# Twenty transposes of the identity matrix on TensorE before the first tile of a two-layer attention and expert kernel

## The chip, the core and the metric

The kernel runs on one core of one Trainium2 chip. The metric is the device time of one execution in microseconds (us); less is better. The times given are medians of several executions, and the profile is of one further execution whose own time is given beside them.

The core has five engines with an instruction stream each: TensorE (PE; its weight loads are shown as PEld), VectorE (DVE), ScalarE (ACT), GpSimd (POOL) and SyncE (SP), which here only issues transfers. The engines wait for one another through semaphores.

## The reference, cut to what matters

Four batches of 256 rows of 256 numbers (`x`) pass through two layers. Each layer adds a cross attention over a context of 1601 rows per batch and then a feed-forward step:

```python
x = x + L0_xattn(layernorm(x), ctx, mask)          # softmax(x @ ctx.T / 16, masked) @ ctx
x = x + L0_ffn(layernorm(x), Wr, Wg, Wu, Wd)       # 8 experts, the best 2 of each row
x = x + L1_xattn(layernorm(x), W_qkv, W_o, ..., ctx, ctx, 54)   # keeps the 54 largest scores of a row
x = x + L1_ffn(layernorm(x), w1, w2)               # rows and weights rounded to few levels
```

Everything is float32 but the last step's products, which are of small integers.

## The kernel before

The 1024 rows are 8 tiles of 128, two tiles to a batch. All work is cut into named steps, and one hand-made list, `ORDER`, gives the order in which they are issued; each engine's block walks the same list (`STEPS`) and issues the steps that are its own. So each engine's order is fixed, and what it does next waits for semaphores alone.

The first steps of the list are the place of this case. SP issues `ldx.0` (x of tiles 0 and 1, L448), the four pieces of the first batch's transposed context (`ldk.1.0.0` to `ldk.1.0.3`, L464, tile `k_sb`, one of 402, two of 400 and one of 399 columns), the other three pairs of x tiles and then the context rows `v_sb` (L480). POOL writes the constants, the identity matrix `ident` among them (L497 to L525), and adds to the semaphore `consts` after each. DVE takes the mean and variance of the first two tiles (`stats`, `aggr`, `var`: L990, L996, L1002), POOL raises the variance to -1/2 (`rstd`, L534) and DVE writes the normalized rows `xn` (`norm.1.0`, L1015). TensorE transposes `xn` into a PSUM bank (`xT.1.0`, L811, tile `T`, four transposes), ACT copies that out (`xTe`, L593), and TensorE multiplies it with the context.

These products are the steps `s1.t.c` (L826): tile t of x with piece c of `k_sb`, into one of the two banks `S`. One such step is two products of 128x128 by 128x400, each of which the trace shows as two MATMUL instructions, so it has four. DVE takes a bank out with the mask added and the row's maximum (`s1e`, L1026, tiles `row` and `mx1c`); after that the bank is free for the step after the next. Ahead of its first `s1e` DVE's order has the statistics of all other x tiles (`stats.1.3`, `stats.1.1`, `stats.1.2`, and what follows them), and between `s1e.0.0` and `s1e.0.1` it has `norm.1.1`.

TensorE's block begins with a wait for all constants (`pe.wait_ge(consts, N_CONSTS)`), and then walks the list. The bank `O_bank` (tile `O`) is first used by `router.0` (L867), tens of us later, whose product overwrites it.

Of the kernel before, what the change touches and what calls it, by code (L numbers as in the profile page):

```python
# [18 lines left out]
P = 128  # L19
# [192 lines left out]
def two_layers(nc, x, ctx, ctxT, mask, Wr, Wg, Wu, Wd, WqT, WoT, beta_q, beta_k, gate, log_tau, w1T, w2T, out):  # L212
    es = ExitStack()
    with es:
        def sb(name, shape, dt=F32):
            return es.enter_context(nc.sbuf_tensor(name, shape, dt))
# [34 lines left out]
        ident = sb("ident", [P, P])  # L251
# [68 lines left out]
        def bank(name):  # L320
            return es.enter_context(nc.psum_tensor(name, [P, 512], F32))
# [3 lines left out]
        O_bank = bank("O")  # L325
# [412 lines left out]
        def _(pe):  # L738
# [59 lines left out]
                    pe.wait_ge(aTe_done, n("aTe", before_t))  # L798

            pe.wait_ge(consts, N_CONSTS)  # L800
            for step in STEPS:
                op, key = step[0], step[1:]
                if op == "xT":
# [544 lines left out]
```

## Time and profile before

| | |
|---|---|
| median of 3 runs | 454.04 us (453.79 to 455.31) |
| the profiled execution's own time | 452.51 us |
| its span, first to last instruction | 450.8 us |
| mean granted TensorE clock in it | 0.943 of full speed |
| PE busy | 359.8 us (80% of the span) |
| PEld busy | 287.6 us (64%) |
| DVE busy | 306.5 us (68%) |
| ACT busy | 172.7 us (38%) |
| POOL busy | 48.8 us (11%) |

The profiled execution has 1.7 us outside its span. PE is busy nearly all the time in the first 40% of the span, DVE from there to the end. In the chain of waits, which is followed back from the last instruction, PE has 36% of the span, DVE 33%, and transfers 9%.

The granted clock is a share of full speed: 1.00 is 2.4 GHz and 0.50 is 1.2 GHz. Busy time of PE is modelled where matmuls are pipelined: what one MATMUL takes by itself is more than the distance between the starts of two in a row.

### The profile page before, as it was taken

How to read it: one execution, taken by the hardware profiler on the slowest of the kernel's cores; microseconds unless marked ns; L12 is line 12 of the kernel's file. 1: busy time of each engine (PE TensorE's matmuls, PEld its weight loads, DVE VectorE, ACT ScalarE, POOL GpSimd, SP SyncE). 2: the span in 40 equal slices, each digit the busy share in tenths (PEclk: the TensorE clock that was granted, in tenths of full speed). 3: DMA queues.
4: the chain of work that ended last, by engine and by line, in shares of the span. 5: the costliest groups of instructions: out<-in, count | busy, mean ns of one | idle time of the engine just before them, and what ended most of it. 6: DMA issues, size and time to landing. Idle time of an engine off the chain costs nothing.

```text
span 450.8 us, 6595 instructions
## 1 busy us (share of the span) xinstructions
PE 359.8 (80%) x2077; PEld 287.6 (64%) x2082; DVE 306.5 (68%) x776; ACT 172.7 (38%) x294; POOL 48.8 (11%) x100
## 2 busy tenths in 40 slices
PE   0999999997999986399998789579958446567975
PEld 0577776875888775286777678477636336556853
DVE  2623474643201341063999999999999999999994
ACT  2143444432432352043433635315663110551475
POOL 3100000034000006440000000271000000000100
PEclk9999999999899999799999999969996958699899
DMA  7593968239187769763989674433421005144201
GB/s 249 173 310 98 310 224 296 84 103 358 37 281 211 236 229 316 245 224 96 321 258 293 191 231 159 133 107 123 125 68 54 0 0 153 45 142 140 82 15 58
DMA packets 70809, 76.38 MB, mean 169 GB/s; under 512 B 5356, under 2 KB 69496, under 8 KB 70776
## 3 DMA queue, kind: packets, MB, share of 16 engines
q1 hardware_dynamic: 57272, 59.93, 41.6%
q10 hardware_dynamic: 11968, 11.84, 8.0%
q0 software_dynamic: 1536, 4.20, 2.7%
q8 instruction: 17, 0.28, 0.2%
q14 instruction: 16, 0.13, 0.1%
HBM read 66.91 MB, written 9.04 MB: 169 GB/s over the span
## 4 chain that ended last, share of the span: by engine, by line
PE 36%; DVE 33%; issue 12%; DMA 9%; POOL 4%; ACT 4%; SPq 1%; ACTq 1%; POOLq 0%; DVEq 0%
PE S L826 11%; PE GU L904 8%; DVE fold L1190 7%; DVE cand_h L1178 7%; PE A L853 5%; PE O L913 4%; DVE cand_l L1185 4%; DMA xg<-xs 3%; DVE fold L1195 3%; DVE row L1218 3%; DMA xs<-xn,idx_u 2%; POOL xs L544 2%; DMA x_res<-x 2%; PE T L840 2%; DVE gabs L1296 2%
## 5 line engine op out<-in xcount | busy, mean ns | idle before, releaser
L904 PE MATMUL GU<-xgT,ew_ring 128*128 128x128 f32 x480 | 60.9, 281 | 9.1 <-issue 8.1
L857 PE MATMUL A<-pT,v_sb 128*128 128x128 f32 (+1 forms) x416 | 59.3, 304 | 10.2 <-ACT pT L608 5.8
L904 PEld LDWEIGHTS GU<-xgT,ew_ring 128*128 128x128 f32 x480 | 58.1, 196 | 13.7 <-issue 9.1
L857 PEld LDWEIGHTS A<-pT,v_sb 128*128 128x128 f32 (+1 forms) x416 | 56.9, 218 | 13.5 <-issue 7.6
L608 ACT ACTIVATE pT<-T 128x512 f32<-128x512 f32 x64 | 31.8, 514 | 87.6 <-PE T L840 85.7
L840 PE MATMUL T<-ident,row 128*128 128x128 f32 (+1 forms) x208 | 34.9, 302 | 32.3 <-DVE row L1218 27.0
L1178 DVE MAX8 cand_h<-fold 128x8 f32<-128x801 f32 x56 | 54.7, 985 | 0.1
L840 PEld LDWEIGHTS T<-ident,row 128*128 128x128 f32 (+1 forms) x208 | 27.6, 156 | 40.5 <-issue 31.0
L853 PE MATMUL A<-v_sb,pT 128*128 128x256 f32 (+1 forms) x208 | 50.7, 388 | 0.0
L826 PE MATMUL S<-k_sb,xT 128*128 128x400 f32 (+2 forms) x128 | 49.0, 516 | 1.3 <-ACT xT L593 1.1
L826 PE MATMUL S<-k_sb,qT 128*128 128x400 f32 (+2 forms) x128 | 45.8, 503 | 2.6 <-ACT qT L665 2.1
L1190 DVE MATCH_REPLACE8 fold<-cand_h,fold 128x801 f32<-128x801 f32 x48 | 46.9, 978 | 0.0
L1117 DVE TENSOR_TENSOR hid<-hid,GU 128x256 f32<-128x256 f32 x30 | 12.4, 416 | 46.0 <-ACT hid L622 45.9
L853 PEld LDWEIGHTS A<-v_sb,pT 128*128 128x128 f32 (+1 forms) x208 | 39.0, 196 | 6.9 <-issue 0.2
L1026 DVE CUSTOM_DVE_ANT_0 row<-S,mask_add 128x400 f32<-128x400 f32 (+2 forms) x32 | 18.3, 573 | 30.3 <-PE S L826 30.2
L826 PEld LDWEIGHTS S<-k_sb,qT 128*128 128x128 f32 x128 | 23.5, 192 | 18.3 <-ACT gel L704 2.3
L913 PE MATMUL O<-ew_ring,hid 128*128 128x256 f32 x120 | 31.6, 385 | 4.0 <-DVE hid L1117 3.2
L826 PEld LDWEIGHTS S<-k_sb,xT 128*128 128x128 f32 x128 | 23.9, 196 | 16.7 <-issue 3.6
L1185 DVE MAX8 cand_l<-fold 128x8 f32<-128x801 f32 x32 | 31.4, 982 | 0.0
L622 ACT ACTIVATE hid<-GU 128x256 f32<-128x256 f32 x30 | 11.5, 384 | 45.8 <-PE GU L904 45.8
L561 POOL TENSOR_TENSOR rstd<-var,minus_half 128x1 f32<-128x1 f32 x8 | 4.6, 579 | 209.6 <-DVE var L1247 209.6
L676 ACT ACTIVATE row<-S 128x400 f32<-128x400 f32 (+2 forms) x32 | 16.0, 504 | 28.2 <-PE S L826 28.2
(153 smaller groups left out, 469.8 us busy)
## 6 DMA issues: line engine op xcount, KB each, us to landing
v_sb<-ctx SPq DMA_DIRECT2D x36, 512.0 KB, 4.1
ew_ring<-Wg SPq DMA_DIRECT2D x30, 256.0 KB, 3.4
ew_ring<-Wu SPq DMA_DIRECT2D x30, 256.0 KB, 3.9
ew_ring<-Wd SPq DMA_DIRECT2D x30, 256.0 KB, 4.5
k_sb<-ctxT SPq DMA_DIRECT2D x16, 400.0 KB, 4.2
xg<-xs ACTq DMA_DIRECT2D x30, 128.0 KB, 3.6
ys<-y_sb ACTq DMA_DIRECT2D x30, 128.0 KB, 3.3
k_sb<-ctxT SPq DMA_DIRECT2D x8, 402.0 KB, 3.9
```

What stands on the lines that cost most here:

```text
L608: act.activation(pT[0:r, i % NPT, :, :].rearrange("p a s -> p (a s)")[:, 0:w], t_bank("pT", *key)[0:r, 0:w], ACT.Copy).then_inc(pTe_done, 1)
L676: act.activation(row3[:, t % 4, c0:c0 + w], s_bank("s3", t, c)[:, 0:w], ACT.Copy) \
L826: mm = pe.matmul(s_bank(*step)[:, 0:w], lhs[:, k, :], k_sb[:, l // 2, c, k, 0:w], start=k == 0, stop=k == KC - 1)
L840: mm = pe.transpose(t_bank(*step)[0:r, a * P:(a + 1) * P], src[:, m * P:m * P + r], ident[:, :])
L853: mm = pe.matmul(A_bank[:, 0:D], pT[0:r, j, a, :], v[0:r, a, :], start=m == 0, stop=m == NMC - 1)
L857: mm = pe.matmul(A_bank[:, o * P:(o + 1) * P], v[0:r, a, o * P:(o + 1) * P], pT[0:r, j, a, :], start=m == 0 and o == 0, stop=m == NMC - 1 ...
L904: mm = pe.matmul(gu_bank(*key)[:, a * F + f * P:a * F + (f + 1) * P], ew_ring[:, w % NW, a, k, f * P:(f + 1) * P], cols[:, k, :], start=k ...
L913: mm = pe.matmul(O_bank[:, 0:D], hid[:, i % NHID, f, :], ew_ring[:, w % NW, 2, f, :], start=f == 0, stop=f == F // P - 1)
L1026: dve.tensor_tensor_reduce(out=row1[:, t % 2, c0:c0 + w], in0=s_bank("s1", t, c)[:, 0:w], in1=mask_add[:, c0:c0 + w], scale=1.0, scalar=BE ...
L1178: dve.max(cand_h[:, t % 2, 8 * r:8 * r + 8], fold[:, t % 2, 0:HALF]).then_inc(maxH_done, 1)
L1185: dve.max(cand_l[:, t % 2, 1 + 8 * r:9 + 8 * r], fold[:, t % 2, HALF:RW]).then_inc(maxL_done, 1)
L1190: dve.match_replace(part, cand_h[:, t % 2, 8 * r:8 * r + 8], part, BELOW_ALL).then_inc(repH_done, 1)
```

## The change

Between TensorE's wait for the constants and its first step, twenty transposes of `ident` are issued, each with `ident` as the second operand too, all into the first 128 columns of `O_bank`. Nothing reads what they write, they wait for nothing more, and they signal nothing. Every other instruction of every engine is as before and in the same order.

```diff
             pe.wait_ge(consts, N_CONSTS)
+            for _ in range(20):
+                pe.transpose(O_bank[:, 0:P], ident[:, :], ident[:, :])
             for step in STEPS:
```

The head of TensorE's instructions before (S is a bank of scores, T one of transposes):

```order
L811 MATMUL T<-ident,xn 128x128 x4
L826 MATMUL S<-k_sb,xT 128x402 x2
L826 MATMUL S<-k_sb,xT 128x400 x4
L826 MATMUL S<-k_sb,xT 128x399 x2
L826 MATMUL S<-k_sb,xT 128x402 x2
```

And after the change, two lines further down in the file:

```order
L802 MATMUL O<-ident 128x128 x20
L813 MATMUL T<-ident,xn 128x128 x4
L828 MATMUL S<-k_sb,xT 128x402 x2
L828 MATMUL S<-k_sb,xT 128x400 x4
L828 MATMUL S<-k_sb,xT 128x399 x2
```

Only the row at L802 is new. Here a product counts once where the trace shows two MATMULs; a transpose is one in both.

## Rows read from the trace of the kernel before

**Rows 1.** The chain that ended last, its start: start us, us, what.
```profile
4.49 8.73 DMA x_res<-x
...
13.24 1.42 DVE bn L990 x4
...
15.21 1.35 POOL rstd L534 x2
...
16.59 0.74 DVE xn L1015 x2
17.32 0.48 DVE row L1026
...
17.87 6.99 PE S L826 x20
```

**Rows 2.** Timeline of PE: start us, us, line, operation, out<-in, count [idle before <-releaser].
```profile
9.65 1.09 PE L811 MATMUL T<-ident,xn 128*128 128x128 f32 x4 [9.65 <-DVE xn L1015]
11.52 6.17 PE L826 MATMUL S<-k_sb,xT 128*128 128x402 f32 x12 [0.78 <-ACT xT L593]
17.87 6.99 PE L826 MATMUL S<-k_sb,xT 128*128 128x399 f32 x20 [0.18 <-DVE mx1c L1026]
24.70 0.60 PE L811 MATMUL T<-ident,xn 128*128 128x128 f32 x4
...
25.98 1.15 PE L840 MATMUL T<-ident,row 128*128 128x128 f32 x8 [0.25 <-ACT xT L593]
```

**Rows 3.** Timeline of the weight loads (PEld), first score steps.
```profile
12.32 0.34 PEld L826 LDWEIGHTS S<-k_sb,xT 128*128 128x128 f32 x1 [0.33 <-issue]
12.99 0.34 PEld L826 LDWEIGHTS S<-k_sb,xT 128*128 128x128 f32 x1 [0.33 <-issue]
...
14.33 0.34 PEld L826 LDWEIGHTS S<-k_sb,xT 128*128 128x128 f32 x1 [0.33 <-issue]
14.88 0.53 PEld L826 LDWEIGHTS S<-k_sb,xT 128*128 128x128 f32 x2 [0.21 <-issue]
16.08 0.97 PEld L826 LDWEIGHTS S<-k_sb,xT 128*128 128x128 f32 x4 [0.68 <-DVE mx1c L1026]
```

**Rows 4.** Timeline of the other engines, 0 to 24 us.
```profile
1.30 1.86 SPq L464 DMA_DIRECT2D k_sb<-ctxT  x3
...
4.07 0.10 POOL L525 MEMSET row<- 128x4 f32 x1
...
10.77 0.60 ACT L593 ACTIVATE xT<-T 128x512 f32<-128x512 f32 x1 [3.34 <-PE T L811]
...
15.44 0.58 DVE L1026 CUSTOM_DVE_ANT_0 row<-S,mask_add 128x402 f32<-128x402 f32 x1
...
17.24 0.57 DVE L1026 CUSTOM_DVE_ANT_0 row<-S,mask_add 128x400 f32<-128x400 f32 x1
```

**Rows 5.** L811, 9 to 11 us: count, duration ns min/median/max.
```profile
L811 PE MATMUL T<-ident,xn x4: 421/421/447, 9.7 to 10.3; 128*128 128x128 f32 x4
```

**Rows 6.** L811 again, 24 to 26 us.
```profile
L811 PE MATMUL T<-ident,xn x4: 271/272/273, 24.7 to 25.0; 128*128 128x128 f32 x4
```

**Rows 7.** All engines, 9.5 to 14.9 us: busy (count) PE, PEld, DVE, ACT, POOL, clock.
```profile
9.50:14.90 5.40, 4.47 (x10) 2.59 (x11) 2.80 (x12) 0.60 (x1) 0.70 (x1) 1.00 1.08 375
```

**Rows 8.** PE stretches around 366 us: length, busy (count), granted clock, DMA, GB/s.
```profile
359.49:366.32 6.83, 0.00 (x0) 0.50 0.00 0
366.32:369.73 3.41, 2.86 (x13) 0.50 0.00 0
369.73:373.14 3.41, 1.97 (x18) 1.00 0.10 16
```

**Rows 9.** Timeline of PE in the middle one of these stretches.
```profile
366.87 2.89 PE L840 MATMUL T<-ident,row 128*128 128x128 f32 x12 [12.65 <-DVE row L1218]
369.56 2.04 PE L857 MATMUL A<-pT,v_sb 128*128 128x128 f32 x16
```

**Rows 10.** PE stretches around a fall of the clock, and one without.
```profile
414.10:417.52 3.42, 1.61 (x15) 1.00 0.47 146
417.52:420.93 3.41, 3.41 (x16) 0.50 0.03 10
400.45:403.86 3.41, 1.37 (x9) 1.00 0.42 148
403.86:407.28 3.42, 2.01 (x16) 1.00 0.00 0
```

**Rows 11.** Transfers issued in the first 10 us: count, KB, us to landing.
```profile
k_sb<-ctxT SPq DMA_DIRECT2D x2, 400.0 KB, 7.3
```

## What the change should do to the time

> **What bounds the kernel now.** I read the chain of waits first, from its start, since the change acts only there. Its start isn't TensorE's [rows 1]: the chain goes through the transfer of later x tiles (it ends at 4.49 + 8.73 = 13.2 us), DVE's statistics of them, POOL's `rstd`, DVE's second `xn`, DVE's second `row` at 17.32, and only at 17.87 does it pass to PE. From there on PE has twenty MATMULs in a row and then goes on with transposes and products with hardly a gap [rows 1, 2]: an idle time of 0.25 us is all that stands before 25.98. So what happens on PE ahead of 17.87 counts only by what it moves the start at 17.87, and every us that is taken from PE after it is on the path.
>
> Second, PE's own rows show how fast it ran. The first four transposes take a median of 421 ns each, and four of the same shape at 24.7 us take 272 ns [rows 5, 6]. The loads of the first score step start 0.67 us apart (12.32, 12.99, and on to 14.33), while the twenty MATMULs from 17.87 take 6.99 us, or 0.35 each [rows 2, 3]. At 14.88 two loads stand in one row, and that is where the pace changes. PE was therefore at the lower of its two clocks (1.2 GHz) when it began at 9.65, and got the higher (2.4 GHz) near 14.8, after it had multiplied without a break from 11.52. The profile's own figure for the granted clock is 1.00 over this whole stretch [rows 7], from before its first recorded change, and does not show this; the durations do. The change gives PE something to do in a time in which it had nothing (it sat idle for 9.65 us [rows 2]), which could bring that rise forward.
>
> Third, what PE waits for between 15.9 and 17.87. The loads of the third score step wait at 16.08 for DVE's `mx1c`, after 0.68 us of idleness, and the fourth step waits for it again at 17.87 [rows 2, 3]. DVE for its part begins `row` at 15.44 without any idle time before it [rows 4]: it came from the statistics, not from waiting for PE's product.
>
> **The change part by part.** The transposes begin when the last constant is written, at 4.07 + 0.10 us [rows 4], say 4.2. Their pace at the lower clock comes from twelve transposes of this shape at a granted clock of 0.50: 2.89 us in all [rows 8, 9], of which the last one's own length is about 0.43, so (2.89 - 0.43) / 11 = 0.22 us apart. The first tile's four give the same: (1.09 - 0.42) / 3 = 0.22 [rows 2, 5]. Twenty end at 4.2 + 19 x 0.22 + 0.43 = 8.8 us. The first real transposes are released at 9.65 by DVE's `xn` [rows 2]. They are covered by PE's own idleness with 0.85 us left over, and cost nothing. Between the bounds for their cost: at the higher clock eight such transposes take 1.15 us [rows 2], so twenty end by 7.1; if each had to end before the next could begin, at 421 ns apiece, they would end at 4.2 + 20 x 0.42 = 12.6 and hold up the first tile by 3.0 us. I take 0.22, since both rows with transposes in a row at the lower clock show it; what is new here is that all twenty write the same columns, for which no row of transposes stands, though the two halves of a product follow one another into the same columns without a gap. The twenty weight loads are of the same kind as those of the other transposes and are in the 0.22.
>
> What they can give. If the clock is high by 9.65 and stays, the four transposes take 0.60 in place of 1.09 (a gain of 0.5 us) [rows 2], and the five spacings between 11.52 and 14.88 shrink from 0.67 to 0.34 or 0.35, which is 5 x 0.33 = 1.6 us. Together 2.1 us of PE's time. Followed through: transposes end near 10.2, ACT's copy of 0.60 us [rows 4] near 10.9, products start at 11.0, and the eight MATMULs of the first two steps are done by 11.0 + 8 x 0.35 = 13.8 instead of about 15.9. The context pieces are there (the two of 400 columns take 7.3 us to land from issues between 1.3 and 3.2 us [rows 4, 11]).
>
> What becomes of it. At 13.8 both `S` banks are full. The third step needs the first one emptied, which DVE does at 15.44 to 16.0, since it is still waiting for x from memory until 13.2 and then working through it [rows 1, 4]. So PE waits from 13.8 to 16.08 where it waited 0.2 to 0.7 us before; the third step begins at 16.08 as before, the fourth at 17.87 as before, because DVE's second `row` comes after `xn`, which comes after POOL [rows 1]. The 2.1 us are gained ahead of a gate that does not move. Sum on the path: 0.0 us. The profiled execution would stay at 452.5 (450.8 of span and 1.7 around it), and scaled to the median of the runs shown that is 454.04 + 0 = 454.0 us.
>
> **Does a transpose raise the clock at all?** At 366 us the granted clock is 0.50 after 6.83 us with nothing on PE; then twelve transposes run and hardly anything else, and in the next stretch the clock is 1.00 [rows 8, 9]. So a row of transposes has been followed by a rise in this very trace. The Trainium skill, page "TensorE: Matmul & The Clock Gate", section "Part 4: PE-mode transpose", says otherwise: that transposes do not count as PE being busy and that the full clock does not engage for them. By that rule the change would leave the clock as it was and the time at 454.0; by the row the clock rises and the time is, through the gate at DVE, 454.0 too. The row speaks against the rule, though the one or two products at the end of that stretch leave a little room for it.
>
> **The rivals.**
>
> *The clock falls in the new gap, slower.* With the first two steps done at 13.8, PE does nothing from 13.8 to 16.08 and works 1.35 us of the next 1.8. The trace has a stretch with 1.61 us of work in 3.42 after which the clock was 0.50, and one with 1.37 in 3.41 after which it was still 1.00 [rows 10]. Before the change the slower pace itself filled this gap. If the clock falls here, it does so near 16 to 18 us and lasts a stretch such as the 3.41 us at 0.50 in rows 10; PE is then on the path, and a half of that is lost: 1.7 us, so 455.7. It decides from the point at which the low stretch reaches beyond 17.87; one that ends before costs nothing. For it: the gap is 2.3 us long and ends right at the place that counts. Against: it needs the rise to have held from 9 to 13.8 first, over the pauses at 8.8 to 9.65 and 10.2 to 11.0; where the clock falls again in these, PE is back to the pace of before and there is no gap.
>
> *Executions differ, and others lose more at the start, faster.* The profiled execution took 452.51 us, 1.5 less than the median. If in others the rise comes later than 14.8, the first eight MATMULs end at 11.52 + 8 x 0.67 = 16.9, and the next four at the lower pace at 19.6, so that the fourth step starts 1.7 us later than 17.87. The change would return up to that, which gives 452.3. For it: the difference of 1.5 us between the profile and the median has no other explanation in the rows. Against: one profile shows one moment of the rise, nothing says that the median run differs just here, and the clock changes in many other places of the program. A part of it, 0.3 to 0.8 us, is likelier than all, and that ends within my "same".
>
> *All 2.1 us arrive.* This would need the gate at 16.08 to be PE's. It gives 451.9. DVE's start at 15.44 with no idle time before it speaks against it.
>
> *The transposes are not over in time, slower.* At 0.42 us each, the first tile's transposes end 3.0 us later, near 13.2 to 13.7, products begin near 14.5 and the first two steps end at 14.5 + 8 x 0.35 = 17.3 or, at the lower clock, 19.9, where the third should have begun at 16.08. That is 1.2 to 3.8 us more: 455.2 to 457.8. It decides from a spacing of (9.65 - 4.2) / 20 = 0.27 us. The slack of DVE's gate forgives a further part of a us.
>
> *It does not do what it says.* The clock rises at the same place as before, by either of two ways: transposes do not count, or the clock is down again by 11 us. The time is 454.0, the same as in my forecast; only the trace tells them apart.
>
> **How the numbers follow.** About 0.3% (1.36 us) is what a measurement of this kernel can tell from no change. My forecast, with the case in which nothing happens to the clock, has 0.70: 454.0, with 453.0 to 455.1 as its own range. Executions that lose more at the start and get back 1.4 us or more: 0.12; all of 2.1 us: 0.03. The clock's fall in the new gap: 0.10, at 455.7; transposes too late: 0.05, at 455.2 or more. So faster 0.15, same 0.70, slower 0.15. For 8 in 10 the range is 452.6 to 455.6, which leaves out the full gain, the late transposes and about a half of each of the two cases at 452.3 and 455.7.
>
> **What the profile after would show.** Twenty transposes of `O` on PE from 4.2 us, 0.22 us apart, faster at the end if the clock rises meanwhile; the last over before 9.65. The four transposes of the first tile at 272 ns each if the clock held, 421 if not. Weight loads of the first score step 0.34 us apart in place of 0.67. PE idle for about 2.3 us until 16.08, released by DVE's `mx1c`. Then the decisive row: twenty MATMULs at 17.87, 6.99 us. A start earlier than 17.6 would prove me wrong on DVE's gate; the same start but 8 us or more for them would be the clock's fall.

## The result

| | kernel before | kernel after |
|---|---|---|
| median | 454.11 us (452.71 to 460.23, 6 executions) | 458.88 us (456.82 to 462.07, 6 executions) |
| ratio after / before, 95% interval | | 1.0115 [1.0066, 1.0165] |
| profiled execution, its span | 452.51, 450.8 us | 461.04, 459.2 us |
| mean granted TensorE clock | 0.943 | 0.926 |

The change costs 4.8 us in this comparison, where 0.0 was forecast. The time lies above the range. The ratios are those on record, which leave out executions in the slow state, here those over 1.5% above the fastest of their kernel. A ratio is therefore not the quotient of the two medians, and differs from it by up to half a per cent. The start of the program, to which the whole prediction was devoted, did what was foretold. The timeline of PE in the profile after, 0 to 27 us (start us, us, engine, line, operation, out<-in, count, idle before and its releaser):

```profile
4.22 4.53 PE L802 MATMUL O<-ident 128*128 128x128 f32 x20 [4.22 <-POOL row L525]
9.57 0.66 PE L813 MATMUL T<-ident,xn 128*128 128x128 f32 x4 [0.82 <-DVE xn L1017]
11.00 2.93 PE L828 MATMUL S<-k_sb,xT 128*128 128x402 f32 x8 [0.78 <-ACT xT L593]
16.05 1.61 PE L828 MATMUL S<-k_sb,xT 128*128 128x400 f32 x4 [2.12 <-DVE mx1c L1028]
17.84 6.99 PE L828 MATMUL S<-k_sb,xT 128*128 128x399 f32 x20 [0.17 <-DVE mx1c L1028]
```

The twenty transposes end at 8.75 us (8.8 was forecast). The first tile's four transposes take 0.66 us in place of 1.09. The first eight MATMULs of the products take 2.93 us, or 0.37 each; before has twelve in one row of 6.17 us, or 0.51 each [rows 2]. Then PE waits 2.12 us for DVE's `mx1c`, and the twenty MATMULs of 17.87 start at 17.84 and take 6.99 us, to a hundredth as before. At 25 us the two kernels stand level.

So the 8.4 us between the two spans arise later. I took the same DVE instruction in both traces (the start of one every few tens of us) and subtracted before from after, and did so for other runs of either kernel too. These differences are counted from the two traces, in us:

| DVE step that before has at (us) | 105 | 118.6 | 152 | 164 | 197 | end of span |
|---|---|---|---|---|---|---|
| after, first profile | 0.0 | 0.0 | 1.9 | 1.9 | 7.6 | 8.4 |
| after, run again (`e14_again2`) | 1.2 | 1.3 | 0.4 | 0.2 | 0.5 | 3.0 |
| before, run again (`e6_control`) | 0.0 | -2.0 | -2.6 | -3.0 | 2.0 | 2.0 |
| before, run again (`e16_control2`) | -0.1 | -2.0 | -2.2 | -2.8 | -3.5 | -1.5 |

Two things are to be seen. Single executions of one and the same kernel part by several us behind 105 us, in the stage where rows of x are gathered and scattered for the experts while PE runs on. And the first profile of after lost most, 5.7 us, between 164 and 197. The waits of that profile (engine, line, waited for: us in total, times, longest) have an entry that before's has not:

```profile
ACT pT L608 <- PE T L842: 84.5, 35, 14.2
...
ACT hid L622 <- PE GU L906: 37.3, 21, 3.3
...
ACT hid L622 <- remote: 9.8, 2, 5.1
```

Its places in ACT's timeline of after:

```profile
181.34 0.38 ACT L622 ACTIVATE hid<-GU 128x256 f32<-128x256 f32 x1 [4.70 <-remote]
184.18 0.38 ACT L629 ACTIVATE y_sb<-O 128x256 f32<-128x256 f32 x1 [2.46 <-remote]
...
203.22 0.38 ACT L622 ACTIVATE hid<-GU 128x256 f32<-128x256 f32 x1 [5.13 <-remote]
```

"Remote" means that the profile holds no instruction whose end released ACT. The products that the first and third of these steps read had ended 2.5 and 3.4 us before, at 178.82 and 199.82, by PE's timeline of after:

```profile
176.80 2.02 PE L906 MATMUL GU<-xgT,ew_ring 128*128 128x128 f32 x16 [0.69 <-issue]
...
197.80 2.02 PE L906 MATMUL GU<-xgT,ew_ring 128*128 128x128 f32 x16 [0.40 <-ACT xgT L615]
```

This is not the change's: the unchanged kernel, run again, has it as well, 2.8 us behind its products. ACT's and PE's timelines of `e6_control`:

```profile
197.65 0.38 ACT L622 ACTIVATE hid<-GU 128x256 f32<-128x256 f32 x1 [4.75 <-remote]
```
```profile
192.56 2.26 PE L904 MATMUL GU<-xgT,ew_ring 128*128 128x128 f32 x16
```

The question for the experiments was therefore double: how much of 4.8 us is the change's at all, and through what, if PE's start is level at 25 us.

### The profile page after: what moved, and what is told of

The parts are those of the page before. It is cut to its first block, busy times and chain, and to the rows that moved or that the text cites. A ratio compares the mean times of both kernels' runs of the same rounds, so it can differ in the third digit from the quotient of the medians.

```text
span 459.2 us, 6634 instructions
## 1 busy us (share of the span) xinstructions
PE 368.7 (80%) x2097; PEld 296.0 (64%) x2102; DVE 306.3 (67%) x776; ACT 172.3 (38%) x294; POOL 48.1 (10%) x100
## 4 chain that ended last, share of the span: by engine, by line
PE 37%; DVE 32%; issue 12%; DMA 8%; ACT 4%; another core or an unknown queue 3%; POOL 2%; SPq 1%; ACTq 1%; POOLq 0%; DVEq 0%
PE S L828 11%; PE GU L906 8%; DVE fold L1192 6%; DVE cand_h L1180 6%; PE A L855 5%; PE O L915 5%; DVE cand_l L1187 3%; DVE row L1220 3%; DMA xg<-xs 3%; PE T L842 2%; DVE fold L1197 2%; PE A L859 2%; DMA x_res<-x 2%; DVE gabs L1298 1%
## 5 line engine op out<-in xcount | busy, mean ns | idle before, releaser
L906 PE MATMUL GU<-xgT,ew_ring 128*128 128x128 f32 x480 | 61.9, 284 | 9.9 <-issue 8.9
L859 PE MATMUL A<-pT,v_sb 128*128 128x128 f32 (+1 forms) x416 | 62.6, 315 | 8.0 <-DMA v_sb<-ctx 5.3
L906 PEld LDWEIGHTS GU<-xgT,ew_ring 128*128 128x128 f32 x480 | 59.2, 199 | 14.6 <-issue 12.0
L859 PEld LDWEIGHTS A<-pT,v_sb 128*128 128x128 f32 (+1 forms) x416 | 60.1, 229 | 11.4 <-DMA v_sb<-ctx 6.1
L828 PE MATMUL S<-k_sb,xT 128*128 128x400 f32 (+2 forms) x128 | 47.4, 503 | 3.4 <-DVE mx1c L1028 2.3
L915 PEld LDWEIGHTS O<-ew_ring,hid 128*128 128x128 f32 x120 | 21.2, 194 | 13.0 <-ACT y_sb L629 7.6
```

The source lines that it names most:

```text
L828: mm = pe.matmul(s_bank(*step)[:, 0:w], lhs[:, k, :], k_sb[:, l // 2, c, k, 0:w], start=k == 0, stop=k == KC - 1)
L859: mm = pe.matmul(A_bank[:, o * P:(o + 1) * P], v[0:r, a, o * P:(o + 1) * P], pT[0:r, j, a, :], start=m == 0 and o == 0, stop=m == NMC - 1 ...
L906: mm = pe.matmul(gu_bank(*key)[:, a * F + f * P:a * F + (f + 1) * P], ew_ring[:, w % NW, a, k, f * P:(f + 1) * P], cols[:, k, :], start=k ...
L915: mm = pe.matmul(O_bank[:, 0:D], hid[:, i % NHID, f, :], ew_ring[:, w % NW, 2, f, :], start=f == 0, stop=f == F // P - 1)
```

## How the experiments are to be read

Kernels were run in five groups, each on one chip with the kernel before beside it, twelve executions of a kernel as a rule. The chips differ: before's median is 455.23, 454.71, 452.82, 452.05 and 452.95 us on them, so a kernel is compared only with before in its own group. Single executions of before scatter with a standard deviation of 2.0 to 2.7 us. Since medians of twelve move by more than a half us for that reason, I give for each run the difference of means to before in us, with its standard error, beside the ratio with its interval. The first difference takes all executions but one of before at 748.83 us, the last only those that the ratio takes. Where the two part, as in `e2_tiny20`, `e5_tiny20b` and `e8_big3`, three or four long executions of twelve make the difference; in `e13_tiny20_mid` and `e17_mid_busy20` it is five long ones of before.

| group, before | kernel | median | ratio, 95% | difference of means, all | the ratio's executions alone |
|---|---|---|---|---|---|
| first comparison, 454.11 | after | 458.88 | 1.0115 [1.0066, 1.0165] | +4.2 ± 1.4 | +4.2 ± 1.4 |
| 1, 455.23 | `e1_again` | 457.16 | 1.0049 [1.0012, 1.0086] | +2.1 ± 0.7 | +2.5 ± 0.6 |
| | `e2_tiny20` | 457.78 | 1.0027 [0.9981, 1.0073] | +2.5 ± 1.1 | +1.3 ± 0.9 |
| | `e3_end20` | 456.44 | 1.0022 [0.9986, 1.0058] | +0.8 ± 0.9 | +0.4 ± 0.7 |
| | `e4_eight` | 454.83 | 0.9999 [0.9963, 1.0035] | -0.1 ± 0.9 | -0.3 ± 0.6 |
| 2, 454.71 | `e5_tiny20b` | 457.30 | 1.0019 [0.9983, 1.0056] | +3.7 ± 1.3 | +1.3 ± 0.6 |
| | `e6_control` | 454.74 | 0.9995 [0.9954, 1.0037] | +0.5 ± 0.9 | -0.3 ± 0.7 |
| | `e7_tiny128` | 456.75 | 1.0026 [0.9991, 1.0061] | +1.5 ± 0.6 | +1.7 ± 0.6 |
| | `e8_big3` | 457.13 | 1.0008 [0.9964, 1.0051] | +2.0 ± 0.9 | +0.6 ± 0.7 |
| 3, 452.82 | `e12_big3b` | 453.28 | 1.0011 [0.9977, 1.0046] | +0.2 ± 0.7 | +0.2 ± 0.7 |
| 4, 452.05 | `e13_tiny20_mid` | 454.94 | 1.0084 [1.0052, 1.0115] | +2.7 ± 0.5 | +3.3 ± 0.5 |
| | `e14_again2` | 453.26 | 1.0029 [0.9993, 1.0066] | +1.4 ± 0.8 | +1.5 ± 0.7 |
| | `e15_tiny20c` | 454.44 | 1.0058 [1.0024, 1.0091] | +2.6 ± 0.8 | +2.6 ± 0.4 |
| | `e16_control2` | 452.22 | 1.0023 [0.9988, 1.0059] | -0.3 ± 0.6 | +0.4 ± 0.6 |
| 5, 452.95 | `e17_mid_busy20` | 452.77 | 1.0034 [0.9993, 1.0075] | +0.2 ± 0.8 | +1.1 ± 0.7 |
| | `e18_mid_big3` | 452.15 | 0.9986 [0.9953, 1.0019] | -1.0 ± 0.7 | -0.1 ± 0.6 |

`e9` to `e11` are short kernels, in their own section.

## Experiments 1: the same again, the instructions without the work, fewer, and elsewhere

`e1_again` is the changed kernel once more. `e2_tiny20` keeps the number of instructions (each `matmul` or `transpose` is a weight load and a MATMUL, so twenty are forty) and takes the array's work out:

```diff
             pe.wait_ge(consts, N_CONSTS)
+            for _ in range(20):
+                pe.matmul(O_bank[0:P, 0:1], ident_h[:, :], ident_h[:, 0:1], start=True, stop=True)
```

`e3_end20` has the twenty transposes behind TensorE's last step:

```diff
                     mm.then_inc(dn_done, 1)
+            for _ in range(20):
+                pe.transpose(S_bank[0][:, 0:P], ident[:, :], ident[:, :])
```

`e4_eight` has eight of them at the start instead of twenty:

```diff
-            for _ in range(20):
+            for _ in range(8):
                 pe.transpose(O_bank[:, 0:P], ident[:, :], ident[:, :])
```

> The changed kernel again, unaltered. Clock theory (C: the early transposes leave the clock's falls later in the program at worse places): slower than before again, ratio 1.008 to 1.015, and the mean granted clock near 0.925 against 0.943. Place theory (L: forty more TensorE instructions at the head shift all that follow, and with that the moments at which later instructions are fetched): the same 1.008 to 1.015. Chance theory (R: executions of both kernels spread by some us, and the runs so far fell apart by luck): ratio 1.000 +- 0.005.

> The twenty transposes are replaced by twenty float16 products of one column, also twenty weight loads and twenty MATMULs, so TensorE's instruction stream has the same length and the same shift, but the array has next to nothing to do and the clock's first rise should stay near 14.8 us. L expects it as slow as the changed kernel, 1.008 to 1.015. C expects 1.000 +- 0.003. R: 1.000 +- 0.005.

> The twenty transposes stand behind TensorE's last step instead of ahead of its first: same program length, nothing ahead of it shifted, nothing early on the array. They lie beside the last ACT, DVE and store work and should cost at most 1 us. L and C both expect 1.000 to 1.002; R 1.000 +- 0.005. If it is slower by 1%, the length of the program or something like it counts, and neither theory holds.

> Eight transposes in place of twenty, at the same place. They take 4.2 to about 6.2 us and should not bring the first rise of the clock forward (it stays near 14.8 us, or where it is in before). The stream is shifted by sixteen instructions. C expects 1.000 +- 0.003; L expects some change of the time, of either sign, up to 1%; R 1.000 +- 0.005.

Measured: the repeat costs 2.1 ± 0.7 us, not 4.8. The products with one column leave the clock of the start alone. PE's timeline of `e2_tiny20`:

```profile
4.22 0.69 PE L802 MATMUL O<-ident_h 128*128 128x1 f16 x20 [4.22 <-POOL row L525]
9.56 1.12 PE L813 MATMUL T<-ident,xn 128*128 128x128 f32 x4 [4.65 <-DVE xn L1017]
11.46 13.38 PE L828 MATMUL S<-k_sb,xT 128*128 128x402 f32 x32 [0.78 <-ACT xT L593]
24.67 0.60 PE L813 MATMUL T<-ident,xn 128*128 128x128 f32 x4
```

Its first tile runs at the lower clock as in before (1.12 us), its next transposes start at 24.67, in before at 24.70 [rows 2], and still its mean is 2.5 ± 1.1 us above before's. Its ratio, 1.0027 [0.9981, 1.0073], isn't clear of 1; of its two repeats below, `e15_tiny20c` is clear of it (1.0058 [1.0024, 1.0091]). What raises the clock at the start is thus not what costs the time. Eight at the start cost nothing that can be measured; twenty at the end are undecided, since they are 2.35 us of work and the bound is as large.

In `e1_again` a part of the loss does lie at the start, and it is the rival that I had priced:

```profile
9.53 0.66 PE L813 MATMUL T<-ident,xn 128*128 128x128 f32 x4 [0.78 <-DVE xn L1017]
10.97 2.93 PE L828 MATMUL S<-k_sb,xT 128*128 128x402 f32 x8 [0.78 <-ACT xT L593]
16.02 9.97 PE L828 MATMUL S<-k_sb,xT 128*128 128x400 f32 x24 [2.12 <-DVE mx1c L1028]
25.83 0.60 PE L813 MATMUL T<-ident,xn 128*128 128x128 f32 x4
```

The clock rose early, fell in the new gap of 2.12 us, and the next transposes come at 25.83 instead of 24.66: 1.17 us on the path.

## Experiments 2: how much is noise, many more instructions, and work with few instructions

`e5_tiny20b` repeats `e2_tiny20`. `e6_control` is the kernel before under a new name. `e7_tiny128` has 128 one-column products instead of twenty, 256 instructions. `e8_big3` makes about as much work for the array with twelve instructions:

```diff
             pe.wait_ge(consts, N_CONSTS)
+            for n_cols in (4, 4, 2):
+                pe.matmul(O_bank[:, 0:n_cols * P], ident[:, :], ident[:, :].unsqueeze(1).to_broadcast([P, n_cols, P]),
+                          start=True, stop=True)
```

> The twenty one-column products again, since their first twelve executions spread from 453.3 to 464.9 us. The place theory (the shifted instruction stream costs time) expects a mean 2 to 3 us above before. The clock theory, in the form that the early rise is followed by a fall at 16 us (1.1 us on the path in the profile of e1_again), expects a mean within 1 us of before, since the products do not raise the clock.

> The kernel before, unaltered, run as if it were a changed kernel. Every theory expects a ratio of 1.000; what it differs from 1 by is the least that a comparison of this size can miss. If it comes out 0.3% or more above, the runs of before and of changed kernels are not of one kind, and the other ratios have to be read against this one.

> 128 one-column products, 256 TensorE instructions in all, over by about 4.2 + 128 x 0.035 = 8.7 us and so ahead of the first tile. The trace shows instructions arriving in blocks of 16384 bytes; if an instruction has 64, that is 256 of them, and the rest of the stream is shifted by just one block. If what counts is where later instructions lie in their blocks, the time is that of before, 1.000. If every added instruction costs, it is worse than e2_tiny20. The clock theory expects 1.000 +- 0.003.

> Three float32 products, two of 512 columns and one of 256, in place of the twenty transposes: the array is busy for about as long (4.2 to 8.5 us), but the stream has only twelve instructions more instead of forty. The clock theory expects the time of the changed kernel, a mean 2 to 3 us above before, with a fall near 16 us in some executions. The place theory expects what eight transposes gave (sixteen more instructions): within 1 us of before.

Measured: the mean of the one-column products is above before's again (+3.7 ± 1.3, or +1.3 ± 0.6 without the long executions), the control's is not (+0.5 ± 0.9). But 256 instructions give 1.5 ± 0.6, not more than forty, so the price does not grow with the number; and the twelve instructions of `e8_big3` gave +2.0 ± 0.9, which its repeat did not bear out (+0.2 ± 0.7). The intervals of all ratios of this group hold 1. A theory by which each added instruction has a price fell here.

## Experiments 3: the first 120 us alone

`e9_short` is the kernel before, cut off behind the first attention; `e10_short_twenty` adds the twenty transposes to it, `e11_short_tiny` the twenty one-column products. The cut:

```diff
+KEPT = ("ldx", "mask", "s1", "s1e", "max1", "exp1", "r1", "x1")
+STEPS = [s for s in STEPS if s[0] in KEPT or s[0] in LAYER1 and s[1] == 1]
+STEPS = [s for step in STEPS for s in ([step, ("store", step[1])] if step[0] == "x1" else [step])]
```

`e12_big3b` repeats `e8_big3`.

> Only the first layer's attention of all eight tiles, from the same list of steps, and a store of x after it; experts, the second attention and the last feed-forward are left out, so its output is not the reference's. It is the base for e10 and e11: the stage up to about 110 us, without the transfers by index that follow. Expected 115 to 125 us with a spread of at most 1.5 us, from the place of the clock's first rise (0 to 0.8 us).

> The short kernel (first attention alone, the rest left out) with the twenty transposes at its head. If the start is where the change costs, this is 1 us or more above e9_short, with the fall of the clock near 16 us that the profile of e1_again showed in most executions. If the cost of the change arises later in the program, this is within 0.4 us of e9_short, of either sign.

> The short kernel (first attention alone, the rest left out) with twenty one-column products at its head, forty more instructions and an idle array. The place theory, if it held for every stage, expects a cost here too; if it works only in the stages left out, or not at all, this is within 0.3 us of e9_short.

> The three large products again (twelve more instructions, a busy array from 4.2 to 8.5 us), as its first twelve executions have a mean of 457.1 with a standard error of 0.8 against 455.3 with 0.3 for all runs of before. If activity ahead of the first tile costs, the mean of both sets stays at 457 to 458; if the forty instructions are what costs, it comes down to 455 to 456.

Measured, five executions each: 123.35 us (123.03 to 124.17), 123.62 (123.08 to 124.31) and 123.62 (122.98 to 123.93); the means are 123.44, 123.60 and 123.54, with standard deviations of 0.35 to 0.46. That is 0.2 ± 0.3 us for the transposes and 0.1 ± 0.3 for the one-column products, up to the end of the first attention; a cost of 2 us isn't there, and neither is the scatter of 2 us and more, which arises behind it. The mean granted clock of `e10_short_twenty` is 0.982 and 0.984 in two executions (123.32 and 124.31 us) and 1.000 in the other three, so the fall in the new gap came in two of five at most. The early rise isn't certain either. PE's timeline of `e10_short_twenty`:

```profile
4.22 4.53 PE L806 MATMUL O<-ident 128*128 128x128 f32 x20 [4.22 <-POOL row L529]
9.34 1.12 PE L817 MATMUL T<-ident,xn 128*128 128x128 f32 x4 [0.59 <-DVE xn L1021]
11.24 13.69 PE L832 MATMUL S<-k_sb,xT 128*128 128x402 f32 x32 [0.78 <-ACT xT L597]
```

Here the same twenty transposes were not followed by the higher clock: the first tile takes 1.12 us.

## Experiments 4: the same instructions at 110 us

In several profiles so far the tensor clock fell near 114 us, after PE had waited for the first gathered rows (`xg`, transposed by the step `xgT.0.0`). `e13_tiny20_mid` puts the twenty one-column products right ahead of that step, into a column of `O_bank` that nothing holds then, so that everything ahead of 109.7 us is as in before:

```diff
                     i = XG_USE[("xgl", *key)]
+                    if key == (0, 0):
+                        for _ in range(20):
+                            pe.matmul(O_bank[0:P, 256:257], ident_h[:, :], ident_h[:, 0:1], start=True, stop=True)
                     t_free(step)
                     pe.wait_ge(xg_in[i % NXG], 16 * (i // NXG + 1))
```

`e14_again2` is the changed kernel, `e15_tiny20c` repeats `e2_tiny20`, `e16_control2` is the kernel before.

> Twenty one-column products stand just ahead of the first transpose of gathered rows (xgT.0.0), where TensorE is idle for 3.4 us in the profile of before (109.9 to 113.3 us) and they take 0.7. All instructions up to there keep their places and all behind are shifted by forty. The place theory expects the cost of the changed kernel, 2 to 4 us above before on this chip. The theory that activity at the start matters expects no cost, 0 +- 1 us.

> The changed kernel a third time, next to e15 and e16 on one chip. If its cost is its own, its mean is 2 to 3 us above e16 and before. If the first two comparisons were scatter between executions, it is within 1 us of them.

> Twenty one-column products at the head a third time. The place theory expects the mean of e14; the theory that a busy array at the start costs expects that of before. The first two sets (24 executions) gave 3 us more than before with a standard error of 0.9.

> The kernel before, unaltered, run as if it were changed. It should agree with before within 1 us; how far it is off says how much the others can be trusted.

Measured: `e13_tiny20_mid` has the clearest cost of the study, 1.0084 [1.0052, 1.0115], +2.7 ± 0.5 us, though nothing ahead of 109.7 us is touched and the array works on one column at a time for 0.64 us. The start is therefore not needed for the loss. PE's timeline of `e13_tiny20_mid`:

```profile
109.66 0.64 PE L887 MATMUL O<-ident_h 128*128 128x1 f16 x20
113.92 0.41 PE L891 MATMUL T<-ident,xg 128*128 128x128 f32 x2 [3.62 <-DMA xg<-xs]
114.17 0.81 PE L811 MATMUL T<-ident,xn 128*128 128x128 f32 x4
114.77 3.41 PE L853 MATMUL A<-v_sb,pT 128*128 128x256 f32 x8
118.02 0.95 PE L867 MATMUL O<-wr_sb,xT 128*128 128x8 f32 x8
118.83 0.41 PE L891 MATMUL T<-ident,xg 128*128 128x128 f32 x2
```

And of the control on the same chip, `e16_control2`:

```profile
112.95 0.41 PE L888 MATMUL T<-ident,xg 128*128 128x128 f32 x2 [3.16 <-DMA xg<-xs]
113.21 0.66 PE L811 MATMUL T<-ident,xn 128*128 128x128 f32 x4
113.70 1.89 PE L853 MATMUL A<-v_sb,pT 128*128 128x256 f32 x8
115.43 0.96 PE L867 MATMUL O<-wr_sb,xT 128*128 128x8 f32 x8
116.24 0.41 PE L888 MATMUL T<-ident,xg 128*128 128x128 f32 x2
```

PE waits 3.62 us for the gathered rows in the one and 3.16 in the other, and then eight MATMULs take 3.41 us in place of 1.89: the clock has fallen. From the first to the second transpose of gathered rows it is 4.91 us against 3.29, so the fall costs 1.6. In six of the eight profiles that have the fall this distance is 4.90 to 4.91 us, in those without it 3.22 to 3.29. In the first profile of after and in `e5_tiny20b` the clock stayed low for two such stretches, and from the first to the third transpose of gathered rows it is 11.22 and 10.57 us, where the control has 7.99: there the fall costs 3.2 and 2.6. The stretches of PE show the fall (from:to, length, PE busy and count, granted clock, DMA share, GB/s), first of `e13_tiny20_mid`:

```profile
114.40:117.80 3.40, 3.40 (x12) 0.50 0.12 39
```

then of `e16_control2`:

```profile
114.40:117.80 3.40, 3.40 (x26) 1.00 0.17 39
```

and of before's first profile, with the wait ahead of it:

```profile
114.40:117.80 3.40, 3.40 (x14) 0.60 0.14 43
```
```profile
113.32 0.41 PE L888 MATMUL T<-ident,xg 128*128 128x128 f32 x2 [3.43 <-DMA xg<-xs]
```

Counted over the 15 profiles of whole kernels of which none fills this wait: with forty more instructions ahead of `xgT.0.0` (after, `e1`, `e14`, `e2`, `e5`, `e15`, `e13`) the clock fell here in 6 of 7, all but `e2_tiny20`; without (before, `e6`, `e16`, `e3`, `e4`, `e7`, `e8`, `e12`, where `e7` has 256, `e4` sixteen, and `e8` and `e12` twelve) in 2 of 8, before's own first profile and `e8_big3`. PE's wait there is 3.47 us on average in the seven and 3.02 in the eight, and 3.44 in those that fell and 2.98 in those that didn't. The length alone doesn't decide: after waits 2.99 us and falls, `e12_big3b` waits 3.27 and doesn't. The grouping was made with the profiles in sight, and each profile is one execution, so this is a lead; the next group tests it.

The same fifteen profiles show where the groups part. By DVE's steps, counted as in the table above, the seven stand on average 0.3 ± 0.3 us behind the eight at 105 us, 2.6 ± 0.6 at 130, 2.3 ± 0.8 at 164 and 2.9 ± 1.3 at the end (chips are mixed here). What the forty instructions cost has thus arisen, on average, by 130 us, in the stretch that has these waits; what comes behind it can't be told from scatter.

A second place shows in three of the seven and in none of the eight: a wait for gathered rows near 131 us. The profiles of after, `e15_tiny20c` and `e13_tiny20_mid` have, each in its own timeline of PE,

```profile
131.81 0.41 PE L890 MATMUL T<-ident,xg 128*128 128x128 f32 x2 [1.49 <-DMA xg<-xs]
```
```profile
131.25 0.41 PE L890 MATMUL T<-ident,xg 128*128 128x128 f32 x2 [1.54 <-DMA xg<-xs]
```
```profile
130.72 0.41 PE L891 MATMUL T<-ident,xg 128*128 128x128 f32 x2 [1.36 <-DMA xg<-xs]
```

where the control has

```profile
127.03 0.41 PE L888 MATMUL T<-ident,xg 128*128 128x128 f32 x2 [0.25 <-DMA xg<-xs]
```

This is 1.1 to 1.3 us more. In these three alone the fetch of a block of instructions (16384 bytes, queue q8) begins between 127.8 and 128.9 us, while the transfer was under way; in the other twelve the nearest is at 129.7. Added instructions shift such fetches: one comes at 108.8 us in `e13_tiny20_mid`, at 114.2 in the control. That both come together in three profiles is all there is for it; no run separates them.

## Experiments 5: filling the wait at 110 us

If the clock's fall after the wait for gathered rows carries the cost, forty instructions at that same place must cost nothing once they keep the array at work. `e17_mid_busy20` puts the twenty transposes there, into a bank not in use; `e18_mid_big3` puts three products of 512 columns there, twelve instructions:

```diff
+                    if key == (0, 0):
+                        for _ in range(20):
+                            pe.transpose(GU_bank[0][:, 0:P], ident[:, :], ident[:, :])
```
```diff
+                    if key == (0, 0):
+                        for _ in range(3):
+                            pe.matmul(GU_bank[0][:, 0:4 * P], ident[:, :],
+                                      ident[:, :].unsqueeze(1).to_broadcast([P, 4, P]), start=True, stop=True)
```

> Twenty transposes of the identity where e13 had its one-column products, ahead of xgT.0.0; at the higher clock they take 2.2 us of TensorE's 3.2 idle ones. Same shift of all that follows as in e13. If the clock's fall near 114 us is what the shift brings, the granted clock stays 1.00 there and the mean is 1 to 2 us below that of e13, that is 0.7 to 1.7 us above before. If the shifted instructions cost in other ways only, it is 2.7 us above before like e13.

> Three float32 products of 512 columns at the same place, 2.6 us of work in twelve added instructions. If the fall at 114 us is the cause and small shifts are harmless, this is 0 to 1 us below before (which has the fall in some executions). If it is above before by 1 us or more, either small shifts cost too or the work itself delays the first gathered tile.

PE's timeline of `e17_mid_busy20`, and its stretch:

```profile
110.30 2.35 PE L887 MATMUL GU<-ident 128*128 128x128 f32 x20
114.38 0.41 PE L891 MATMUL T<-ident,xg 128*128 128x128 f32 x2 [1.73 <-DMA xg<-xs]
114.63 0.60 PE L811 MATMUL T<-ident,xn 128*128 128x128 f32 x4
115.06 1.89 PE L853 MATMUL A<-v_sb,pT 128*128 128x256 f32 x8
116.79 0.95 PE L867 MATMUL O<-wr_sb,xT 128*128 128x8 f32 x8
117.60 0.42 PE L891 MATMUL T<-ident,xg 128*128 128x128 f32 x2
```
```profile
114.40:117.80 3.40, 3.40 (x24) 1.00 0.11 39
```

and of `e18_mid_big3`:

```profile
109.69 2.74 PE L887 MATMUL GU<-ident 128*128 128x512 f32 x6
114.70 0.41 PE L892 MATMUL T<-ident,xg 128*128 128x128 f32 x2 [2.27 <-DMA xg<-xs]
...
117.92 0.41 PE L892 MATMUL T<-ident,xg 128*128 128x128 f32 x2
```

The clock stays at 1.00 in both, and it is 3.22 us from the first transpose of gathered rows to the second. Forty instructions at the same place that cost 2.7 ± 0.5 us with the array idle cost 0.2 ± 0.8 with the array busy: 2.5 ± 0.9 between them, from two chips, each against before on its own. By the ratio's executions alone it is 3.3 ± 0.5 against 1.1 ± 0.7, 2.2 ± 0.9 between them, and a cost of 1 us may remain. With twelve instructions the mean is 1.0 ± 0.7 us below before's, and the ratio 0.9986 [0.9953, 1.0019], which can't be told from no change.

So filling the wait takes most of the cost away. That it does so through the fall of the clock fits these two profiles, but one number on record speaks against the clock as the whole cause. One stretch of 3.41 us at half pace lowers the mean granted clock of an execution by 0.0037, and falls in 6 of 7 in place of 2 of 8 executions would lower a kernel's mean by 0.0023. Over all executions the mean of `e13_tiny20_mid` is 0.9321 ± 0.0010, and that of before on its chip 0.9308 ± 0.0009; `e1`, `e2`, `e5`, `e13`, `e14` and `e15` together (72 executions) differ from before by -0.0003 ± 0.0007. Either the fall at 114 us is not so frequent as the profiles make it seem, or the clock fell less elsewhere. The filled kernels are 0.0079 ± 0.0019 and 0.0070 ± 0.0017 above before, which is more than one stretch.

## Why the prediction was wrong

**The pace, the end and the cover of the transposes: right.** 0.22 us apart, over at 8.75 us, 0.82 us of idle time left of the 0.85 forecast. The row of twelve transposes [rows 8, 9] was the right one to go by.

**The clock: right, though not in each execution.** The first tile at the higher clock after twenty transposes is in the profiles of after, `e1_again` and `e14_again2`; with eight transposes, with one-column products and in `e10_short_twenty` it isn't. The Trainium skill, page "TensorE: Matmul & The Clock Gate", section "Part 4: PE-mode transpose", by which transposes don't bring the full clock, is contradicted by three of these traces: 0.66 us for the first four transposes against 1.09 to 1.12 without.

**The gate at DVE: right.** Start at 17.84 (17.87 before), 6.99 us (6.99), and a gap of 2.12 us ahead of 16.05 (about 2.3 forecast). All that was gained on PE was lost there.

**The fall in the new gap: right in kind, too dear and too rare.** Its chance was given as 0.10; it came in two of three profiles of the changed kernel (`e1_again`, `e14_again2`). Its price was given as 1.7 us and is 1.17 in `e1_again` and 1.23 in `e14_again2` (next transposes at 25.89). The term was mis-sized by taking half of a whole stretch as lost: between 16.05 and 17.84 there are four MATMULs, 4 x 0.34 = 1.4 us of work in 1.8, and these 0.4 us of slack take a part of the half pace. Over executions it is worth 0.2 ± 0.3 us, by the short kernels, if these can stand for the whole.

**Everything behind 17.87 as before: wrong.** This is the step that failed. The sum said 0.0 because at 17.87 the two kernels are level, "every other instruction as before", and I asked of no later wait whether it was stable. It is not: near 110 us PE waits about three us for gathered rows, before's own profile shows the clock's fall behind it (its stretch 114.40 to 117.80 has a granted clock of 0.60), and whether it falls varies between executions. What the runs show in place of 0.0 is a loss that has arisen by 130 us: forty instructions right ahead of this wait cost 2.7 ± 0.5 us with nothing ahead of 109.7 us touched, and 0.2 ± 0.8 when they keep the array at work. I read rows on falls of the clock at 400 and 414 us [rows 10] and did not ask which of them are coin tosses that a small shift can load. In the profiles with forty more instructions ahead of this place the wait is longer by about 0.45 us and the fall more frequent. Falls in 6 of 7, worth 2.1 us on average (1.6 to 1.7 in four, 2.6 and 3.2 in two), against 2 of 8 at 1.6 to 1.7 make 1.4 us; the wait near 131 us, 3 of 7 at 1.2 us, is 0.5; both together 1.9 us. This is an estimate from single profiles. Twenty transposes at the start cost 2.1 ± 0.5 us over their three comparisons (30 executions; 2.3 ± 0.4 by the ratio's executions), the one-column products 2.8 ± 0.6 (36; 2.0 ± 0.3). The sum fits, but since the mean clock of whole executions doesn't bear out the frequencies, the share of the clock's fall in the loss is argued and not shown.

**A spread of 0.3%: wrong.** It came from three executions, 453.79 to 455.31. Thirty-five executions of before lie between 448.06 and 457.34 us on one chip, the standard deviation is 2.2 us. My range of 3.0 us allowed for none of this, and the rival on executions that differ looked for the difference at the start, where five executions of `e9_short` lie within 1.1 us. The difference of 1.5 us between the profiled execution and the median was no sign of a loss at the start; two executions differ by that as a rule.

**The size of the first result.** Repeats gave +2.1 ± 0.7 and +1.4 ± 0.8, so that more than half of the 4.8 us didn't come again, and the first profile had two waits of ACT of 4.70 and 5.13 us of the kind that the control shows as well.

**What stays open.** Why the wait for gathered rows is longer behind forty added instructions, when their time itself is hidden. Fetches of instruction blocks fit the second place, but 256 added instructions (+1.5 ± 0.6, no fall at 114) fit no simple form of it. At the first place they show no pattern: the nearest fetch begins at 108.5 to 109.8 us in `e5`, `e13`, `e17` and `e18` and at 113.9 to 116.8 in all others, and both sets hold profiles with and without the fall. A small part of the cost lies outside the span: the time of an execution less its span is 1.74 to 1.76 us on average in before and in all whole kernels with none, twelve, sixteen or 256 more instructions or with forty at the end, and 1.88 to 2.05 us in all those with forty more at the start or at 110 us, `e17_mid_busy20` among them. No run says why. Whether twelve instructions at the start cost anything (+0.8 ± 0.6 over both runs) isn't settled either. And filling the wait was tried only at 110 us, not in the kernel that has the transposes at the start, so that this fill would cure the changed kernel is argued and not shown.

## What to carry to other kernels

An edit whose time is fully hidden can still cost half a per cent far behind its place. The likeliest way here is a wait of PE behind which the clock falls in some executions and not in others: list such waits in the profile, ask of each whether it is the same in a second execution, and price the edit there as well. Before a warm-up is put ahead of the first work, look for what releases the second and third step; if that is another engine, the gain ends at it, and the new gap can let the clock fall again. Measure the kernel before against itself first: here a control of twelve executions was good to 0.6 to 0.9 us, and a result from six was off by two.

## What the runs showed of the chip that I had not expected

- Forty TensorE instructions with next to no array work cost 2.5 ± 1.1, 3.7 ± 1.3 and 2.6 ± 0.8 us at the start (1.3 ± 0.9, 1.3 ± 0.6 and 2.6 ± 0.4 by the ratio's executions) and 2.7 ± 0.5 us at 110 us, while their own time was 0.69 and 0.64 us beside idle time; sixteen at the start gave -0.1 ± 0.9, and two controls 0.0 ± 0.5 together.
- The falls of the clock differ from execution to execution of one kernel: at 114.4 to 117.8 us the granted clock was 0.60 in before's first profile and 1.00 in both repeats.
- In the stage with gathers and scatters ACT started 2.5, 3.4 and 2.8 us after the recorded end of the products that it reads, in changed and unchanged kernels, and the profile names no instruction that released it. What holds it up wasn't looked into.
- The granted clock in the records is 1.00 for the first stretches whatever the engine does: in `e10_short_twenty` the first tile's transposes take 1.12 us, in after 0.66, and the records show 1.00 in both. At the start only durations tell the pace.
